# Attention heads gathered by DMA and normalised feature by token, expert sums kept feature by token, gates turned on TensorE and spread by DMA

## The reference

```python
Q = rope(x @ qw); K = rope(x @ kw); V = x @ vw            # 2 x 1024 tokens, 16 heads of 8
score = einsum("bhqd,bhkd->bhqk", Q, K) / sqrt(8) - 1e10 * (1 - causal)
score = score - max(score)
attn = softmax(score) @ V
x = layernorm(x + merged(attn) @ ow)
probs = softmax(x @ router_w + router_b);  top_p, top_i = top_k(probs, 2)
gates = zeros.at[top_i].add(top_p / sum(top_p))            # tokens x 4 experts
h = silu(x @ w1[e]) * (x @ w3[e])                          # e = 0..3, width 512
out = sum_e gates[:, e] * (h @ w2[e])
x = layernorm(x + out)
```

## Time and profile before

| what | value |
|---|---|
| median of 3 runs | 412.04 us (410.81 to 413.67) |
| time of the profiled execution | 413.73 us |
| its span, first to last instruction | 412.0 us |
| PE busy | 386.8 us (94%) |
| DVE busy | 310.0 us (75%) |
| ACT busy | 260.8 us (63%) |
| POOL busy | 208.2 us (51%) |
| mean granted PE clock | 0.977 of full speed |

### The profile page before, as it was taken

How to read it: one execution, slowest core, us unless ns; L and a number is a source line. 1 busy time by engine, 2 the same in 40 slices (tenths; PEclk the granted TensorE clock), 3 DMA queues, 4 the chain that set the end, 5 groups by cost and what they waited for, 6 DMA issues and landing times.

```text
span 412.0 us, 7446 instructions
## 1 busy us (share of the span) xinstructions
PE 386.8 (94%) x2402; PEld 203.3 (49%) x2424; DVE 310.0 (75%) x1022; ACT 260.8 (63%) x373; POOL 208.2 (51%) x274
## 2 busy tenths in 40 slices
PE   6897979999999999999999998999999999999992
PEld 2441232323323233232332434888888888888780
DVE  2869799899999999999999761455586568656653
ACT  1361527686866868668686687666566756666560
POOL 7177478542614436044360422756476546755662
PEclk9996889999999999999999999999999999999997
DMA  7474011375232232322310000000000000000000
GB/s 233 160 216 95 0 22 29 88 237 173 55 94 45 47 82 55 95 45 46 85 27 3 3 1 2 0 2 1 2 1 25 2 1 27 2 0 2 25 2 25
DMA packets 46164, 21.14 MB, mean 51 GB/s; under 512 B 30379, under 2 KB 44331, under 8 KB 46126
## 3 DMA queue, kind: packets, MB, share of 16 engines
q1 hardware_dynamic: 42718, 18.44, 17.1%
q10 hardware_dynamic: 3408, 2.23, 1.8%
HBM read 13.11 MB, written 7.35 MB: 50 GB/s over the span
## 4 chain that ended last, share of the span: by engine, by line
PE 80%; DVE 10%; ACT 3%; issue 3%; DMA 2%; POOL 1%; POOLq 0%; SPq 0%; ACTq 0%; DVEq 0%
PE o_bank L1264 16%; PE bank L1338 11%; PE t_bank L1338 11%; PE bank L1223 10%; PE t_bank L1351 10%; PE t_bank L1246 8%; PE small_bank L1223 5%; DVE maxima L960 2%; DVE x_w L956 2%; PE o_bank L1360 2%; PE t_bank L1176 2%; ACT num L766 1%; DVE mg_w L956 1%; DMA wqk<-in_kw 1%; DVE mg_t L956 1%
## 5 line engine op out<-in xcount | busy, mean ns | idle before, releaser
L766 ACT ACTIVATE num<-t_bank 128x1024 f32<-128x1024 f32 (+2 forms) x160 | 141.9, 940 | 65.3 <-PE t_bank L1246 65.2
L659 POOL TENSOR_TENSOR hid_lo<-num,q_op 128x512 fp32r<-128x512 f32 x63 | 81.8, 1302 | 57.7 <-ACT q_op L830 56.5
L621 POOL TENSOR_SCALAR_AFFINE_SELECT num<-num 128x512 f32<-128x512 f32 x64 | 40.2, 638 | 102.2 <-ACT num L766 101.9
L1264 PE MATMUL o_bank<-num,v_op 128*32 128x512 f32 (+3 forms) x768 | 80.1, 497 | 0.1
L1223 PE MATMUL bank<-k_op,q_op 128*128 128x512 bf16 (+7 forms) x241 | 65.3, 327 | 3.4 <-DVE maxima L956 1.3
L830 ACT ACTIVATE q_op<-num 128x512 fp32r<-128x512 f32 x64 | 40.5, 632 | 42.6 <-DVE num L1104 42.1
L960 DVE TENSOR_REDUCE maxima<-bank 128x1 f32<-128x512 f32 x83 | 55.3, 684 | 2.0 <-PE bank L1223 0.8
L1246 PE MATMUL t_bank<-q_op,k_op 64*128 64x512 bf16 (+3 forms) x384 | 49.4, 334 | 3.7 <-ACT num L766 1.3
L1104 DVE TENSOR_TENSOR num<-bank,num 128x512 f32<-128x512 f32 x32 | 22.1, 691 | 34.3 <-ACT num L837 34.0
L1223 PEld LDWEIGHTS bank<-k_op,q_op 128*128 128x128 bf16 x257 | 20.7, 98 | 53.9 <-DVE maxima L960 21.8
L1104 DVE TENSOR_TENSOR num<-t_bank,num 128x512 f32<-128x512 f32 x32 | 22.1, 690 | 26.3 <-ACT num L837 24.0
(11 more groups left out here) (162 smaller groups left out, 654.6 us busy)
## 6 DMA issues: line engine op xcount, KB each, us to landing
q_op<-q_scratch SPq DMA_DIRECT2D x64, 48.0 KB
w_raw<-in_w_all SPq DMA_DIRECT2D x6, 512.0 KB, 4.0
k_op<-k_scratch SPq DMA_DIRECT2D x28, 96.0 KB, 2.2
xT<-in_x_feat SPq DMA_DIRECT2D x4, 256.0 KB, 6.0
x_res<-in_x_tok ACTq DMA_DIRECT2D x4, 256.0 KB, 3.1
q_scratch<-num SPq DMA_DIRECT2D x2, 384.0 KB, 2.8
k_scratch<-num SPq DMA_DIRECT2D x2, 384.0 KB, 2.9
out_tokens<-num SPq DMA_DIRECT2D x3, 256.0 KB, 2.3
```

What stands on the lines that cost most here:

```text
L621: pool.affine_select(out=tile, in_=tile, compare_op=ALU.is_ge, fill=0.0, base=0, pattern=[[0, GH], [1, P]], channel_multiplier=-1)\
L659: pool.tensor_tensor(hid_lo[:, m % HB, :], hid[:, m % HB, :], hid_hi[:, m % HB, :].bitcast(F32), ALU.subtract).then_inc(f_lo, 1)
L766: act.activation(num[:, t % PB, :, off:CH].rearrange("p (k i) t -> p i k t", i=2)[:, :, h:h + each, :], t_bank[k % TB][:, :, 0:each * (CH ...
L1264: ins = pe.matmul(o_bank[h * QD:(h + 1) * QD, off:CH], v_op[w][:, kt, h, :], num[:, t % PB, h, off:CH], start=kt == 0, stop=kt == TI * (c ...
```

## The change

1. The step NORM is gone, with its transposes, reciprocals and multiplications. V's block of ones is 8 columns wide, so a head's tile holds its 8 features and 8 equal rows of sums. `o_sb` is now two tiles of 1024 tokens, one for each group in turn, and SP gathers each head by DMA: 8 rows of results into `o_all` (the space of `xT`) and 8 rows of sums into `den_all`, 8 transfers for a group (`gather_heads`).
2. For each chunk DVE takes the reciprocal of 128x512 sums and multiplies (r = 0), which gives `mg_t` feature by token at once; `mg_w` and its transposes are gone.
3. Experts' sums stay feature by token: DVE multiplies the sum in PSUM with `gate_rows` and adds it to `sum_t`, which starts from `x1_tw`. PE turns the total once per chunk (`TR_STEP` = 19); statistics and normalisation read PSUM.
4. The gates of a chunk are turned on PE (16x128), copied by DVE to `gates_t`, stored to DRAM and read back spread over all partitions, one transfer for each expert (`spread_gates`).
5. The pieces between chunks start at unit 3 instead of 7 (`NEXT_AT`), so pieces 0 to 3 of chunks 2 and 3 stand in steps 19 to 22, beside the statistics of the chunk that ends.
6. In the last chunk all normalisation is on DVE.
7. Prologue: the first loads are spread over both queues with `xT`'s first chunk in two halves, a third warm-up matmul is added, the unturned projections no longer wait for the turned weights, DVE forms all four sums of turns, and the loads of `k_op` for group 0 are on SP instead of ACT's queue.
8. The two strings of order lose their n and are written anew.

```diff
-STEADY_ORDER = "ssmttssspssttsspssttsspsstspsttssspmsttsssptsspssttssspssttsspssttsspsnttnpp"
+STEADY_ORDER = "sstsmtssspsttssspssttssppssttsspmssttsspssttsspssttssspssttsspssttsspsttpp"
...
+NEXT_AT = E_LAST
+def next_steps(n, i):
+    r = n - NEXT_AT
+    return [(i + 1 + r // UNITS, r % UNITS)] if i + 1 + r // UNITS < CHUNKS else []
...
+            def gather_heads(n):
+                b, g = divmod(n, NG)
+                sp.wait_ge(o_copied, 1 + NC * (n + 1))
+                for h in range(GH):
+                    for k, dst in enumerate((o_all, den_all)):
+                        at, rows = g * QD + h * DH, h * QD + k * DH
+                        sp.dma_start(dst[at:at + DH, b * S:(b + 1) * S], o_sb[n % 2][rows:rows + DH, :])\
...
+            def spread_gates(ch):
+                sp.wait_ge(g_copied, ch + 1)
+                sp.dma_start(g_dram[ch, :, :].rearrange("e (t p) -> (e t) p", p=P), gates_t[:, :]).then_inc(g_stored, 16)
+                sp.wait_ge(g_stored, 16 * (ch + 1))
+                for e in range(E):
+                    sp.dma_start(gate_rows[ch % 2][:, e, :], g_dram[ch, e, :].partition_broadcast(P))\
...
+                if r == 0:                                      # DVE
+                    b, at = ch // NC, slice(ch * CH, (ch + 1) * CH)
+                    for i in range(2):
+                        dve.wait_ge(heads_in[b][i], 16 * GH * NG)
                     dve.wait_ge(c_y, 1 + ch)
+                    dve.reciprocal(den_all[:, at], den_all[:, at]).then_inc(c_mg, 1)
+                    dve.wait_ge(c_mg, ch + 1)
+                    dve.tensor_tensor(mg_t[:, :], o_all[:, at], den_all[:, at], ALU.mult).then_inc(c_mgs, 1)
...
+                if r == 1:                                      # PE
+                    pe.wait_ge(c_mgs, ch + 1)
...
+                    dve.wait_ge(g_loaded[ch % 2][e], 16 * (ch // 2 + 1))
+                    dve.wait_ge(f_w2, ch * UNITS + FT * (e + 1) + HB)
+                        dve.tensor_tensor(gated[:, e % 2, half], bank[4 + e % 2][:, half], gate_rows[ch % 2][:, e, half],
+                                          ALU.mult).then_inc(f_eo, 1)
...
+                        dve.tensor_tensor(sum_t[:, half], gated[:, e % 2, half], (sum_t if e else x1_tw)[:, half],
+                                          ALU.add).then_inc(f_y, 1)
```

More of the change, by code:

```diff
@@ L510, in _ @@
                     .then_inc(out_stored, 16)
+            for s in range(1, GROUPS + 1):
+                stage(STAGES[s], s, s % 2, load=s < GROUPS - 1)
+            for ch in range(0, CHUNKS):
+                spread_gates(ch)
+                if ch == 0:
+                    continue
+                store_out(ch - 1)
+            store_out(CHUNKS - 1)
             sp.wait_ge(out_stored, 16 * (CHUNKS + 1) + 16)
@@ L675, in _ @@
                 experts(0, n)
+                for step in next_steps(n, 0):
+                    between(*step)
             for i in range(0, CHUNKS - 1):
@@ L991, in stage @@
                         experts(0, step[1])
[L993 to L998 removed]
+            for s in range(GROUPS):
+                stage(STAGES[s], s)
             def statistics(src, step_sem):
@@ L1137, in experts @@
                     dve.wait_ge(f_rstd, ch + 1)
-                    normalise(lambda i: y_sb[:, i, :], lambda i: z_sb[:, i, :], f_z,
-                              TI // 2 if ch == CHUNKS - 1 else TI)
+                    for k, half in enumerate(halves(ch, E - 1)):
+                        normalise(lambda i: bank[6 + k][:, i * D:(i + 1) * D], lambda i: z_sb[:, i, :], f_z,
+                                  y_mv, y_rstd, range(half.start // P, half.stop // P))
             dve.wait_ge(ld_small, 16 * 6)
             dve.wait_ge(ld_res, 16 * CHUNKS)
-            stage(LAST, GROUPS, last_base)
+            stage(LAST, GROUPS)
             for n in range(E_LAST, HEAD):
                 experts(0, n)
+                for step in next_steps(n, 0):
+                    between(*step)
             for i in range(0, CHUNKS - 1):
```

375 lines of the change are left out of this document (155 added, 220 removed).

## The result

| | before | changed |
|---|---|---|
| median, us | 412.86 (410.81 to 413.83, 4 runs) | 431.44 (429.85 to 435.41, 4 runs) |
| span of the profiled execution, us | 412.0 | 428.1 |
| last copy of `o_sb` of stage 0 (ACT) | 49.68 | 46.04 |
| stage 1 / stage 2 / stage 3, us | 28.38 / 25.76 / 25.64 | 27.84 / 25.06 / 26.78 |
| each of the stages 4 to 7, us | 25.64 to 25.65 | 24.54 (24.65 in stage 7) |

The ratio is 1.047, with a 95% interval of 1.039 to 1.056: the change makes the kernel slower, where 405.2 us was forecast. The stages are cut at ACT's copies into `o_sb`, which every kernel here makes at the same places of the program. Up to the end of stage 7 the changed kernel is 8.05 us ahead. Stage 8 gives 2.5 of them back, and the expert part 21.7.

The account below looks back on a forecast made before the run. PE was taken to set the pace from about 60 to 402 us, DVE close behind in attention. -8.1 - 3.5 + 0.2 - 7.5 + 9.0 + 3.8 - 0.7 = -6.8 us on 412.04 gave 405.2 us, range 398 to 411.5.

Parts of the forecast that it names:

- attention stages 1 to 7: Each stage loses two NORM groups, 1.16 us of PE, and DVE shrinks as much: -8.1 us over seven stages.
- prologue and stage 0: Earlier first projection and S step, sums of turns on DVE, row transfer ahead of loads: -3.5 us.
- stage 8: Last attention stage: removed PE work was cover, PE waits for `mg_t`, T starts about as before: +0.2 us.
- experts, PE's removed turns: Expert part: 16 groups of turns at 0.505 us go, less three small turns of gates: -7.5 us.
- experts, stalls: Expert part, chunks 1 to 3: PE waits for `mg_t` and then for DVE's late `hid`: +9.0 us.
- experts, clock: Expert part: a half-clock stretch behind each of three stalls, 5.4 us less 1.6: +3.8 us.
- end: After ACT's last copy: gated halves, sums and turns replace copy, turns and eight gated additions: -0.7 us.
- one of the rivals: DVE holds the attention stages: only half of the 8.1 us comes, 409.3 us; chance 0.12.
- X: Stage 8: when DVE's last maximum is done, 230.4 us before; T of the second half could start at X + 7.6.
- The reciprocal: 512 columns on DVE, per chunk: 3.2 us; the rival of 4.4 us gave 410.0 us, chance 0.15.
- The walk through DVE's work: Expert steps 20 to 22, chunks 2 and 3: `hid` of unit 7 ends at 15.6, wanted at 14.8: 0.8 us each.
- that the clock stays low: Rival: after each of three stalls the clock stays low for 10 us, 5.0 instead of 1.8 us: 414.8 us; chance 0.04.

Follow-up runs that it names:

- run 10: Run 7's kernel with four of group 0's gathers left in stage 2 and four behind the first send of stage 3: 409.62 us, 0.989 of before.
- run 12: Run 7's kernel with run 10's gathers and chunk 0's reciprocal in pieces, two ahead of DVE's copy of the rows, two behind: 408.67 us, 0.990 of before.
- run 1: Changed kernel with the four 512-column reciprocals replaced by a plain operation of the same size, division left out: 426.64 us, one execution.
- run 9: Run 7's kernel with chunk 0's reciprocal made in stages 6 and 7, two pieces in each: 408.15 us, 0.986 of before.
- run 5: Changed kernel with the router's piece ahead of the gated sum in DVE's order, same instructions in the same steps: 418.98 us, 1.015 of before.
- run 2: Changed kernel with POOL's `hid_lo` subtraction cut to 64 of 512 columns: 426.02 us, one execution.
- the pieces alone: Changed kernel with the reciprocals of chunks 1 to 3 in four 128-column pieces during the chunk before: 426.16 us, 1.032 of before.
- run 7: Changed kernel with run 5's order and the reciprocals of chunks 1 to 3 in four early 128-column pieces: 408.61 us, 0.990 of before.
- run 11: Run 7's kernel with both run 9's early division of chunk 0 and run 10's shared gathers: 408.26 us, 0.986 of before.
- run 6: Changed kernel with each expert's gating and sum, and what follows them, one step later: 427.65 us, 1.038 of before.
- run 4: Changed kernel with all eight gathers of group 0 moved from stage 2 to behind the first send of stage 3: 432.04 us, 1.045 of before.

## Why the prediction was wrong

The sum, step by step. The last column is the changed kernel against the kernel before, in their profiled executions. The row on the clock is what the other rows leave of the difference.

| step | forecast, us | measured, us |
|---|---|---|
| attention stages 1 to 7 | -8.1 | -4.4 (-0.5, -0.7, +1.1, then 4 x -1.1) |
| prologue and stage 0 | -3.5 | -3.6 |
| stage 8 | +0.2 | +2.5 |
| experts, PE's removed turns | -7.5 | -5.6 |
| experts, stalls | +9.0 | +26.5 |
| experts, clock | +3.8 | about +1.5 |
| end | -0.7 | -0.8 |

**Attention.** 1.1 us for a steady stage against 1.16: right, and PE and DVE shrank together, as argued. Stages 1 and 2 gave 0.5 and 0.7 us; for stage 1 the same code took 26.98 to 28.01 us in other executions, for stage 2 it stays open. That the total is near half of the 8.1 us, as in one of the rivals, is luck: the steady stages gave theirs in full. Stage 3 is the exception. I priced the eight gathers on SP at nothing because of their targets, and I did not name what is queued behind them. SP sent the rows at 103.49 us, PE waited 2.19 us for them until 106.29, and run 10 shows 1.7 us back when half of them is moved.

**Prologue.** The number is right, and only partly for my reasons. See the last section.

**Stage 8.** X is 222.8 us in the changed kernel. The projection began at X + 4.6 (forecast X + 4.1, before X + 3.5), and from 227.9 to 231 us PE ran at half clock, which costs 1.55 us. The step that failed is that T of the second half could start at X + 7.6 by the rows; it started at X + 9.5, since PE was still at the work ahead of it. Run 12 shows that an earlier row transfer changes nothing, and runs 1 and 9 that a stage without the reciprocal takes 21.3 and 20.65 us. I had looked at the clock for the experts, not here.

**Experts, PE.** I took PE's timeline from the first to the last first-layer matmul of the experts, each distance from start to start less 0.231 us where it follows a large matmul. Before, 14 turns of experts' sums take 5.6 us of it, three of `mg_w` 1.2 and a NORM 0.4; in the changed kernel three turns of totals take 1.1 us and the gates 0.4. That is 5.6 us, at 0.40 us a group, where I had 16 groups at 0.505 with the longer matmul behind each. The step is over-sized by 2 us.

**The reciprocal.** 3346 ns against 3.2 us: right, and 4.4 us, which I had estimated from the Trainium skill ("VectorE: DVE Perf Modes", section "First, the fixed hardware budget"), was not what it took.

**Experts, stalls: the step that failed.** By the same reckoning the starts that follow a wait come 26.9 us late, against 0.4 before; the list of waits shown first has 25.1 of them. The stalls at `mg_t` were forecast at 2.8, 2.3 and 2.3 us, 7.4 together, and were 6.8. The walk through DVE's work behind them gave 0.8 us twice. That walk is the step that failed: 15.6 us stood at `x_w`, `hid` and the logits, and 2.3 at the turn of the total. I had listed DVE's instructions in steps 20 to 22 and taken the sum of their durations as the delay. Three things were left out. The gated sum stands ahead of the pieces 3, 7 and 11 in the order, and the old chunk's normalisation ahead of piece 3, so results for which another engine waits come later (run 5: 12.5 us). POOL has `hid_lo` queued behind `rstd`, so a late `veps` makes three subtractions pile up. And DVE's own instructions stretch beside this pile, from 1.11 to 3.01 us (run 2: 5.5 us of the wait for `x_w`). I had a row for such stretching, 920 ns beside POOL, and used it for the gated sums only. The normalisation I took as 1.0 us, from plain multiplications, though the trace of the kernel before had one at 2.82 us. None of the rivals was this one. The nearest, that the clock stays low, was about PE alone.

The two causes are apart in PE's waits: the pieces alone take 6.7 us of them away, the order alone 11.5, both 17.5. In the time both bring more than their sum, 22.8 us against 5.3 and 12.5, because only with both does the clock's cost fall, from 15.2 to 11.1 us.

**Clock.** +3.8 us was forecast for one lowered stretch at each of three stalls. The profiled execution of the changed kernel had a single one in the experts (0.71 at 260 to 264 us and 0.86 at 264 to 268), run 5's had two, and run 7's none before 400 us. In the profiles in which a wait of the experts was 2.5 us or longer there were one to four such stretches there; in those of runs 7 and 9 to 12, with 1.3 us as the longest, there was none up to 396 us. So the stretches go with the long stalls, but not one for each, and their cost differs from execution to execution.

**Gates.** They were never waited for, as forecast. The store landed 1.3 us and the spread loads 3.7 to 3.8 us after their issue, against 10.4 us of cover.

**What the change is worth.** Without its two faults of order the change brings a part of what its removed work promised: run 9 is 1.4% (1.1 to 1.8) faster than the kernel before. Run 7, which differs from the changed kernel only in the order and in the reciprocals' cut, is 1.0% faster (0.4 to 1.6). By run 9's profile all of its gain lies ahead of the last copy of `o_sb` (246.51 us against 253.34); the part behind it takes 159.1 us against 158.7, for 6.8 us of waits stay there and use up the 5.6 us of removed turns. I did not find a way to take those away.

## What to carry to other kernels

When work moves onto an engine with room, write down for each of its instructions which engine waits for the result, and put the ones that are waited for ahead of those that nobody waits for in the next step. The sum of durations does not show this; here the same instructions in the same steps were 12.5 us apart. And price each wait with what is queued behind it: `rstd` was 1 us of POOL's time, but three `hid_lo` stood behind it, and the eight gathers were nothing, but the send of the rows stood behind them.

Read a gain as two sums, the waits that went and what the clock cost in each execution. The reciprocal's pieces brought 5.3 us alone and 10.4 behind the mended order, though they removed about the same waits (6.7 and 6.0 us): the last long stall gone, the lowered clock in the experts went too.

## What was not expected of the hardware

**One-input operations beside GpSimd.** Four DVE `tensor_scalar` operations on 128x128 fp32 in SBUF took 1.11 us and beside three GpSimd subtractions 3.01 us, the longest 1299 ns for one. Small operations are affected as well. In run 5 the `tensor_scalar` of 4 columns at 308.71 us took 1.25 instead of 0.17 us, and GpSimd's subtraction beside it ran from 308.63 for 1.29 us, so both ended within 0.05 us. In run 7 a `scalar_tensor_tensor` of 16 columns took 1.27 us and ended 0.03 us behind one. It doesn't happen to every operation that runs beside GpSimd. The same `tensor_scalar` with its input from PSUM took 394 to 411 ns all 14 times in the changed kernel; in run 6 four of them (315.60 us, 1.35 us) ran beside a subtraction. What decides it was not tried.

**The start of an execution differs in length.** The second pair of projections began at 9.15 to 10.1 us in nine of the profiled executions of the changed kernel and its variants, at 11.17 us in one (run 12), at 11.6 to 11.7 us in three (runs 5, 10 and 11), and at 12.35 in the one of the kernel before. Most of it is still there at the end of stage 0, where the last copy of `o_sb` began at 45.6 to 47.0, at 47.5 and at 48.8 to 49.0 us. Here the changed kernel and run 10, PE's first six fp32 matmuls:

```profile
6.05 2.84 PE L1167 MATMUL t_bank<-xT,wqk 128*128 128x512 f32 x6 [0.83 <-DMA xT<-in_x_feat]
```

```profile
6.67 4.30 PE L1189 MATMUL t_bank<-xT,wqk 128*128 128x512 f32 x6 [1.45 <-DMA xT<-in_x_feat]
```

In all, these six took between 2.84 and 4.71 us, and not by how late they began: in run 4 they began at 6.38 us and took 2.84, in run 12 at 5.77 us and took 4.71. The granted clock of these rows is not resolved enough to show whether it is the clock, and the cause stays open. So up to 2.8 of the prologue's 3.6 us may be this and not the change. With one profiled execution of the kernel before, that stays open too.
